# Storing a batch tile's gathered embedding rows in five transfers instead of one

## The reference

```python
e = jnp.stack([tbl_0[ids[:, 0]], ..., tbl_32[ids[:, 32]]], axis=1)     # (1024, 33, 128)
row, col = np.triu_indices(33, k=1)                                    # 528 pairs
inner = e[:, row] * e[:, col]
fm = relu(einsum('bpd,ad->bpa', inner, attn_W) + attn_b)
attn = softmax(einsum('ba,bpa->bp', gnn_feature, fm), axis=1)
attn_output = einsum('bp,bpd->bd', attn, inner) * 100.0
h = concatenate([gnn_feature, attn_output, gnn_feature], axis=1)
h = maximum(h @ W_top1 + b_top1, 0.0)
h = maximum(h @ W_top2 + b_top2, 0.0)
y = h @ W_top3
```

## Time and profile before

| what | us |
|---|---|
| median of 3 runs | 1270.41 (1270.02 to 1271.27) |
| the profiled execution | 1270.63 |
| span of the profiled execution, first to last instruction | 1268.2 |
| TensorE busy / VectorE busy / ScalarE busy / GpSimd busy | 1201.0 / 1147.9 / 1018.7 / 451.8 |

### The profile page before, as it was taken

The page is one execution under the profiler, slowest core; times in us unless marked ns, Lnnn a source line. Parts: engine busy times, 40 slices in busy tenths (PEclk is TensorE's granted clock), DMA queues, the critical chain, the costliest instruction groups (busy, mean ns, idle before and its releaser), DMA issues.

```text
span 1268.2 us, 20736 instructions
## 1 busy us (share of the span) xinstructions
PE 1201.0 (95%) x8732; PEld 898.7 (71%) x8732; DVE 1147.9 (91%) x649; ACT 1018.7 (80%) x1039; POOL 451.8 (36%) x270
## 2 busy tenths in 40 slices
PE   1499999999999999999999999999999999999998
PEld 1267676777777777777777777677777777777766
DVE  2399899998999989999899989999799998999994
ACT  1288898778987889878897798978888788887883
POOL 6587684018800386005840088201880000000000
PEclk9999999999999999999999999999999999999999
DMA  4211410311103111131101311031110300011001
GB/s 108 97 34 50 105 32 26 102 45 30 34 13 125 31 32 28 30 106 37 32 20 47 106 27 32 20 111 39 30 34 21 117 18 1 1 29 39 17 9 38
DMA packets 54859, 58.83 MB, mean 46 GB/s; under 512 B 10728, under 2 KB 49136, under 8 KB 53744
## 3 DMA queue, kind: packets, MB, share of 16 engines
q1 hardware_dynamic: 46304, 40.20, 10.4%
q0 software_dynamic: 8448, 17.32, 5.2%
q10 hardware_dynamic: 16, 0.00, 0.0%
HBM read 36.12 MB, written 17.31 MB: 42 GB/s over the span
## 4 chain that ended last, share of the span: by engine, by line
PE 83%; ACT 8%; issue 4%; DVE 2%; POOL 2%; another core or an unknown queue 1%; DMA 1%; SPq 0%; ACTq 0%; DVEq 0%; POOLq 0%
PE scores L610 19%; PE ring L580 17%; PE ring L587 13%; PE ring L589 12%; PE ring L588 12%; PE ring L634 4%; ACT fm L308 3%; ACT inner_hi L316 3%; PE ring L620 2%; POOL x_rows L280 2%; PE ring L654 1%; DVE products L418 1%; ACT exp_pairs L323 1%; PE ring L648 1%
## 5 line engine op out<-in xcount | busy, mean ns | idle before, releaser
L308 ACT ACTIVATE fm<-ring,attn_b_sb 128x848 f32<-128x848 f32 (+1 forms) x640 | 597.2, 971 | 183.1 <-PE ring L580 174.3
L418 DVE TENSOR_TENSOR products<-xt 128x2112 f32<-128x2112 f32 x256 | 601.9, 2351 | 37.1 <-ACT xt L347 37.1
L280 POOL DMA_INDIRECT x_rows<-in_tbl,ids_all x264 | 451.1, 1709 | 498.2 <-PE ring L620 408.3
L423 DVE TENSOR_TENSOR low_parts<-products,inner_hi 128x1688 fp32r<-128x1688 f32 (+4 forms) x256 | 467.1, 1825 | 57.1 <-ACT inner_hi L316 56.0
L587 PE MATMUL ring<-inner_hi,attn_wt_lo 128*128 128x424 f32 (+1 forms) x971 | 433.1, 446 | 5.1 <-ACT fm L308 5.1
L316 ACT CAST inner_hi<-products 128x1688 fp32r<-128x1688 f32 (+4 forms) x256 | 392.3, 1532 | 5.2 <-DVE products L418 5.2
L589 PE MATMUL ring<-inner_hi,attn_wt_hi 128*128 128x424 f32 (+1 forms) x971 | 344.1, 354 | 0.0
L588 PE MATMUL ring<-low_parts,attn_wt_hi 128*128 128x424 f32 (+1 forms) x971 | 343.7, 354 | 0.0
L580 PE MATMUL ring<-products,attn_wt 128*128 128x424 f32 (+1 forms) x618 | 275.8, 542 | 10.0 <-issue 6.4
L610 PE MATMUL scores<-fm,gnn_blocks 128*32 128x264 f32 x4096 | 254.6, 389 | 6.5 <-ACT exp_pairs L323 6.4
L587 PEld LDWEIGHTS ring<-inner_hi,attn_wt_lo 128*128 128x128 f32 x971 | 182.6, 188 | 70.8 <-issue 37.6
(11 more groups left out here) (53 smaller groups left out, 203.9 us busy)
## 6 DMA issues: line engine op xcount, KB each, us to landing
x_dram<-x_rows SPq DMA_DIRECT2D x8, 2112.0 KB, 6.6
x_fields<-x_dram SPq DMA_DIRECT2D x128, 128.0 KB
x_rows<-in_tbl,ids_all POOLq DMA_INDIRECT x264
attn_t<-attn_turned SPq DMA_DIRECT2D x124, 32.0 KB, 1.9
w_sb<-in_W_top SPq DMA_DIRECT2D x2, 512.0 KB
x_fields<-in_r_gnn_feature SPq DMA_DIRECT2D x1, 512.0 KB
h<-in_W_top SPq DMA_DIRECT2D x1, 256.0 KB
ids_all<-in_ids SPq DMA_DIRECT2D x1, 132.0 KB, 2.7
```

The costliest lines, as they stand in the source:

```text
L280: nc.gpsimd.indirect_dma_start(out=x_rows[:, f, :], out_offset=None, in_=tables[f], in_offset=bass.IndirectOffsetOnAxis(ap=ids_all[:, t, f ...
L308: nc.scalar.activation(dst, slot(("hidden", pair, j))[:, :, 0:n], ACT.Relu, bias=attn_b_sb[:, 0:1]).then_inc(s_fm, 1)
L418: nc.vector.tensor_tensor(dst, a, b, ALU.mult).then_inc(s_inner, 1)
L423: nc.vector.tensor_tensor(inner[:, S % INNER_BUFS, at:end], plain[:, S % INNER_BUFS, at:end], inner_hi[:, S % HI_BUFS, 0:end - at].bitcast ...
```

## The change

`store_rows(t)` stores each group's fields as soon as that group is gathered, as a transfer of its own with a semaphore of its own: four transfers of 8 fields (512 KB, a run of 4 KB in each partition) and one of 1 field (64 KB). SyncE's wait for a stored tile becomes five waits, `wait_stored`. GpSimd's wait before it gathers a group again is for that group's store alone. The order of the instructions on each queue stays.

```diff
-        s_store = sem("rows_stored")
+        s_store = [sem(f"rows_stored{c}") for c in range(XJ)]
...
             def store_rows(t):
                 for c in range(XJ):
+                    own = slice(FU * c, FU * c + fields_in(c))
                     sp.wait_ge(s_gather[c], 16 * fields_in(c) * (t + 1))
-                sp.dma_start(x_dram[t * P:(t + 1) * P, :, :], x_rows[:]).then_inc(s_store, 16)
+                    sp.dma_start(x_dram[t * P:(t + 1) * P, own, :], x_rows[:, own, :]).then_inc(s_store[c], 16)
+
+            def wait_stored(t):
+                for c in range(XJ):
+                    sp.wait_ge(s_store[c], 16 * (t + 1))
...
-            sp.wait_ge(s_store, 16)
+            wait_stored(0)
...
-                sp.wait_ge(s_store, 16 * (t + 2))
+                wait_stored(t + 1)
...
                     if t > 0:
                         pool.wait_ge(s_xt_done, XJ * (t - 1) + c + 1)
-                        pool.wait_ge(s_store, 16 * t)
+                        pool.wait_ge(s_store[c], 16 * t)
```

## The result

The change makes the kernel slower: 1304.89 us against 1270.69, a ratio of 1.0271 with a 95% interval of 1.0257 to 1.0284. The profiled execution took 1305.04 us, its span 1302.6, 34.4 more than before. I had forecast 1267.9.

What follows compares the result with a forecast made beforehand. TensorE, busy 1201.0 of 1268.2 us, bounds the kernel, so only the start could gain: 2.73 us stall less 0.2 left gives 2.5, other terms 0. Median 1270.41 - 2.5 = 1267.9 us, range 1267.2 to 1270.8.

Steps and rivals of the forecast that it cites:

- the cover for the first part, GpSimd's wait: Tile 1's gather moves ahead, but no wait for rows exists beyond tile 0, so worth 0; uncovered, at most 8.59 us.
- The shift of the gather's first transfer: Tile 1's first gather moves from 54.63 to 46.04, right behind tile 0's last gather: 8.59 us earlier.
- The reading of the start: Job 3's copy, 2.73 us late at 50.91, was held by store 0; smaller parts leave 0.2 us, gaining 2.5.
- The coincidence at 48: At the start, the stall begins where store 0's 2.1 MB transfer begins, while the last matmuls reading the same buffer finish.
- the stall stays: Rival at the start: the late release is something of TensorE's own, not the transfer; time 1270.4, chance 0.28.
- The first had transfers of parts 0 to 2 slow down the gathers: Slower rival in the first 46 us: job 3 3.9 us late, time 1271.8, or 1274.3 without the gain; chance 0.05.
- The second had SyncE fall behind: Slower rival in the loop: SyncE's issues and waits take over 10.2 us instead of 3.6; chance 0.01.
- a cover of 10.2: SyncE's queue waits 10.2 us between tile 2's store and the next load, covering 3.6 us more issuing: worth 0.
- Five stores in pieces cost nothing: In the main loop, storing in pieces costs nothing; a transfer up to 5.3 us longer is covered by 10.2 us.
- the earlier loads of fields: Tile 0's fields are loaded some 8 us sooner, for a job at step 7 of tile 1: worth 0.
- the later tiles' waits: From tile 2 on, GpSimd's wait for the store never binds, the transposition being the later condition: worth 0.
- the transposition jobs start as foreseen: Tile 0's jobs begin at 15.86, 26.07, 35.99 and 46.19; beginning later would prove the forecast wrong.

Runs made afterwards that it cites:

- e2: Kernel before, with its one store of tile 0 issued only when the first product is made: 1270.03 us, ratio 0.9998.
- e1: Changed kernel with its five stores, but GpSimd starts tile 1's gather only when the first product is made: 1270.01 us, ratio 0.9999 to the kernel before.
- s1: e1 plus one GpSimd memset pause of about 0.5 us behind field 15 of tile 0: 1269.72 us, ratio 0.9998.
- e4: Kernel before, with 16 spare indirect gathers by GpSimd right behind tile 0's: 1293.19 us, ratio 1.0178.
- p1: Changed kernel, with VectorE also waiting for each transposition job of tile 0 and then doing a small memset: 1294.43 us.
- p3: Kernel before, with 16 added matmuls of 128 columns behind each transposition job of tile 0, results not used: 1317.94 us.
- r2: Kernel before, with 16 plain loads of 64 KB issued by GpSimd behind tile 0's gather: 1269.81 us, ratio 0.9998.
- r4: e1 plus one GpSimd memset pause of about 1 us behind field 15 of tile 0: 1269.35 us, ratio 0.9996.
- r3: Kernel before, with 16 plain loads of 64 KB issued by SyncE once tile 0 is gathered, ahead of the store: 1270.41 us, ratio 1.0035.
- p4: Kernel before, with 20 GpSimd memsets of 4 KB in each partition behind tile 0's gather, issuing no transfer: 1286.00 us.
- s3: Kernel before, with 16 spare indirect gathers of 32 rows instead of 128 behind tile 0's: 1325.00 us.
- s2: Kernel before, with 16 spare indirect gathers behind tile 0's, every index 0 so all rows are one DRAM row: 1294.70 us.

## Why the prediction was wrong

**The step that failed** is the cover for the first part, GpSimd's wait: "none of it reaches the end ... Worth 0". I costed the early gather by who waits for its rows, found nobody, and did not ask what 33 more gathers do to the engines beside them while the start is still on the chain. They cost 34.4 us: 15.1 until the first product and 19.3 in the first steps. The wait for store 0 had been an unintended pause for TensorE, and the diff took it away. The shift of the gather's first transfer was right (8.59 us foreseen, 8.93 measured), but the gather ended 28.5 us sooner, at 94.6 instead of 123.1, because beside an idle VectorE it keeps the quick pace; so tile 0's fields are loaded 28 us sooner, at 97.16 instead of 125.14, and not some 8.

**The reading of the start.** The coincidence at 48 was read as the 2.1 MB store's holding the result, worth a gain of 2.5 us. e2 shows that the store has no part in it: the term is 0. There was a second coincidence that I had in hand: GpSimd's last gather ends at 45.74, and in before, e1, e2 and s1 job 3 follows 4.5 to 5.2 us later. I had named "the stall stays" with 0.28, on the ground of TensorE itself; the stall did not stay, it grew, and I had no rival in which the early gather disturbs an engine.

**The slower rivals.** The first had transfers of parts 0 to 2 slow down the gathers. They did not: three of the four jobs start up to 0.4 us earlier than before. The second had SyncE fall behind; the five issues took 4.39 us where one took 0.45, 3.9 us more against a cover of 10.2.

**What held.** Five stores in pieces cost nothing (e1); the earlier loads of fields and the later tiles' waits change nothing that the trace shows (34.35 us late at the first reduction, 34.4 at the end); the transposition jobs start as foreseen.

**Why 34 us and not 3.** The state feeds itself, as far as the traces tell. In the main loop of before, VectorE works without a break, and beside it a gather takes 1.1 to 3.1 us, most often 1.96. Once TensorE is held up, VectorE runs out of work, GpSimd goes back to 0.94 us a gather, and TensorE is held up further; see the gathers at 86.14 and 87.39 and VectorE's 1.48 us of 11 in the window from 79. It ends when the gather does. In the kernel before the same row of gathers ended at 45.7, just when TensorE was needed.

The Trainium skill, in "SBUF — State Buffer", section "Who interferes with whom", says that "PE and ACT never wait on anyone". If that is meant for the SBUF ports alone, no run here contradicts it; as a rule for reckoning what GpSimd can do to TensorE it fails, by 27 matmul records in 29 us against 224.

**What stays open** is the mechanism inside the chip. Shown is that an early or added row of indirect gathers issued by GpSimd does it (changed kernel, e1, e4), that TensorE is the engine held (p1, p3), and that it is back some 5 us after the last gather in p3 and within 2.7 us in the changed kernel. Why plain loads from the same engine do not do it, and by what path a gather reaches TensorE, no run tells.

Nor is it known when it sets in. In p3 it took 23 us of gathers from the start of the program (4.6 to 27.5) and about 9 us in the second row (54.9 to 64). But job 2's copy, at the end of 33 us of gathers, was prompt in some traces (38.0 to 38.9 in before, e1, e2, r2, r4, s1) and 2 to 5 us late in others (40.3 to 43.4). Up to there the kernels before, e4, r2, r3, p4 and s3 do the same, so that their edits do not decide it; it may vary from one execution to the next. Every execution on record has a span and a granted clock from the hardware profiler; whether its recording has a part in the delay, no run can show.

## What to carry to other kernels

A transfer that is moved earlier needs more than a reader who does not wait for it: ask which engines are on the chain at the moment that it moves to, and measure whether its issuing touches them. If GpSimd gathers in a long row, look at how far TensorE's results lie behind its last matmul; where it is microseconds, a wait for the first loop step (e1) takes the large delay away; a pause of a microsecond in the row (r4) took away the small one, 2.7 us, in the one execution traced, with no gain in the median that can be told from none. And a wait whose removal "costs nothing" may be what keeps two things apart; a wait with an unrecognised releaser on the chain is to be explained before anything is built on it.

## What the runs showed of the hardware

- After 23 us of indirect gathers at one each 1.25 us, TensorE's matmul records, which had come each 0.11 to 0.24 us, came mostly each 2.1 or 2.8 us (p3). With 16 more gathers behind tile 0's, job 3 was copied at 62.6 to 63.3 instead of 50.9, whether each gathered 128 rows, 32 rows or the same row 128 times (e4, s3, s2).
- 16 plain loads of 64 KB by GpSimd took it 8.6 us in all, less than half of what 16 gathers take (20 us), and TensorE's job 3 was copied in the midst of them, at 50.69, as in the kernel before (r2).
- A pause of about 1 us in the row, behind the 16th gather, went with a prompt job 3 at the end of the row; one of 0.5 us did not. Each is one trace (r4, s1).
- A single indirect gather took 51.37 us beside a VectorE that never stopped (p4), where the same gather at nearly the same time took 1.79 us in e2 and 1.14 us in r3.
